# Attention of a two-layer block: head pairs on half rows, four heads' values in turn, and a reordered setup

## The reference

```
q = ln(x, lna_w) @ Wq.T + bq;  k = ln(x, lnb_w) @ Wk.T;  v = ln(x, lnb_w) @ Wv.T + bv
# q, k scaled by HD**-0.25 and split into 16 heads of HD = 8
for i in range(3):
    qp, kp, vp = qcur @ lq_w.T + lq_b, k @ lk_w.T + lk_b, v @ lv_w.T + lv_b
    sq, sk = ln(qp, lnc_w) * rsqrt(temp), ln(kp, lnd_w)
    scores = where(pos < cw, sq @ sk.T / sqrt(HD), -inf)
    iter_out = where(row < cw, softmax(scores) @ vp, 0)
    diff = mean(abs(iter_out - prev))            # sets the next window cw and the flags
    qcur = qcur + iter_out;  prev = iter_out
output = attn @ Wo.T + bo
```

## Time and profile before

| what | value |
|---|---|
| three runs | 592.22, 596.55, 597.31 us |
| median | 596.55 us |
| the profiled execution | 597.31 us, its span 595.6 us |
| mean granted clock of PE, share of full speed | 0.756 |
| PE, DVE, ACT, POOL busy | 373.8, 330.7, 180.8, 193.0 us |

### The profile page before, as it was taken

One profiled execution on the slowest core, in us unless ns is written; L12 is line 12 of the kernel. 1 busy time (PEld: TensorE's weight loads), 2 busy tenths in 40 slices (PEclk: granted clock), 3 DMA queues, 4 the chain that ended last, 5 costly groups with the idle time before them and its releaser, 6 DMA issues.

```text
span 595.6 us, 8658 instructions
## 1 busy us (share of the span) xinstructions
PE 373.8 (63%) x2164; PEld 262.0 (44%) x2165; DVE 330.7 (56%) x974; ACT 180.8 (30%) x376; POOL 193.0 (32%) x341
## 2 busy tenths in 40 slices
PE   1843698578981769249578999854506451049890
PEld 0631234424331333013378999843504451048890
DVE  7886797696019683000655555521576988126770
ACT  0020155103530114124225445411653054023540
POOL 8010003778895006730030000375120002714442
PEclk9965598556995558769978999965757855559996
DMA  2995000000000001110012222221153000233320
GB/s 59 272 362 188 0 0 2 1 0 2 0 0 0 0 1 36 53 44 0 10 53 56 60 66 70 71 66 48 40 187 148 1 0 10 100 88 79 77 65 2
DMA packets 36217, 34.55 MB, mean 58 GB/s; under 512 B 6259, under 2 KB 26949, under 8 KB 36192
## 3 DMA queue, kind: packets, MB, share of 16 engines
q1 hardware_dynamic: 32432, 26.83, 14.7%
q0 software_dynamic: 3712, 7.44, 4.4%
q10 hardware_dynamic: 48, 0.00, 0.0%
HBM read 19.92 MB, written 14.79 MB: 58 GB/s over the span
## 4 chain that ended last, share of the span: by engine, by line
PE 39%; issue 22%; DVE 19%; another core or an unknown queue 8%; DVEq 2%; ACT 2%; SPq 2%; DMA 2%; POOL 1%; ACTq 0%; POOLq 0%
PE ps L886 11%; PE ps L1001 8%; PE ps L1012 7%; DVE mx L1488 4%; PE ps L860 4%; PE ps L827 3%; PE ps L875 3%; SPq L284 2%; DVEq L1599 1%; DVE w_now L1604 1%; DVE rs_a L1127 1%; PE ps L991 1%; DMA y<-back,posu 1%; DVE rs_a L1126 1%
## 5 line engine op out<-in xcount | busy, mean ns | idle before, releaser
L460 POOL DMA_INDIRECT rows<-token_rows,posu x48 | 48.4, 1008 | 162.7 <-DVE posu L1419 82.9
L1001 PE MATMUL ps<-xsT,w_now 128*128 128x128 f32 x552 | 82.4, 297 | 23.5 <-issue 14.7
L1612 DVE TENSOR_TENSOR hb<-ps,b_in 128x512 f32<-128x512 f32 x69 | 47.5, 689 | 84.0 <-PE ps L1001 53.2
L886 PE MATMUL ps<-wide,v_now 128*32 128x309 f32 (+2 forms) x256 | 76.1, 440 | 22.2 <-ACT wide L597 10.5
L1001 PEld LDWEIGHTS ps<-xsT,w_now 128*128 128x128 f32 x552 | 73.5, 208 | 29.6 <-issue 17.7
L1012 PE MATMUL ps<-w_out,hg 128*128 x552 | 79.5, 292 | 6.0 <-issue 3.0
L1012 PEld LDWEIGHTS ps<-w_out,hg 128*128 128x128 f32 x552 | 72.7, 206 | 8.1 <-issue 8.0
L679 ACT ACTIVATE hg<-hb 128x512 f32<-128x512 f32 x69 | 43.3, 630 | 49.2 <-DVE hb L1612 46.5
L886 PEld LDWEIGHTS ps<-wide,v_now 128*32 128x32 f32 x256 | 25.7, 116 | 59.8 <-issue 20.6
L1488 DVE TENSOR_REDUCE mx<-ps 128x512 f32 (+2 forms) x48 | 43.5, 948 | 12.1 <-PE ps L860 12.1
L1454 DVE TENSOR_SCALAR den<-ps 128x48 f32<-128x48 f32 (+1 forms) x3 | 0.6, 203 | 87.6 <-PE ps L911 87.6
(11 more groups left out here) (335 smaller groups left out, 584.8 us busy)
## 6 DMA issues: line engine op xcount, KB each, us to landing
rows<-zeros SPq DMA_DIRECT2D x22, 256.0 KB, 6.3
xs<-rows SPq DMA_DIRECT2D x69, 64.0 KB
back<-ys SPq DMA_DIRECT2D x46, 64.0 KB
w_in<-in_L_ffn_w_fc SPq DMA_DIRECT2D x1, 2048.0 KB, 14.1
w_in<-in_L_ffn_W SPq DMA_DIRECT2D x1, 2048.0 KB, 8.5
rest<-rows SPq DMA_DIRECT2D x23, 65.0 KB
token_rows<-in_L_attn_x SPq DMA_DIRECT2D x1, 832.0 KB, 8.1
wmod<-in_L_wmod SPq DMA_DIRECT2D x2, 384.0 KB, 4.4
```

Source lines behind the costliest of these rows:

```text
L460: pool.indirect_dma_start(ROWS[l], bass.IndirectOffsetOnAxis(ap=posu[:, k, j:j + 1], axis=0), token_rows[:, j, 0:WIDTH[l]], None).then_inc ...
L886: mm = pe.matmul(ps[q * OROW:(q + 1) * OROW, 6, 0:nw], v_now[:, q, jk, :], probs[:, q % 2, jk, 0:nw], start=(jk == 0), stop=(jk == nj - 1))
L1001: mm = pe.matmul(ps[:, c % RING, n * P:(n + 1) * P], w_now[:, c % 2, n * P:(n + 1) * P], xsT[:, c % 2, :], start=True, stop=True)
L1612: v.tensor_tensor(hb[:, c % 2, :].rearrange("p (b t) -> p b t", b=NB), ps[:, c % RING, :].rearrange("p (b t) -> p b t", b=NB), b_in[:, l, ...
```

## The change

Keys and queries of a head pair lie on half rows. A head's keys take 64 rows (the head's half of the turned stack) and the scores product reads these alone (`half`); the key buffer holds 8 pairs instead of 16 heads, and isn't cleared first. The maxima are one bf16 number instead of three. The stack is turned by groups of four heads (`turn_group`), and the turns stand between the score products; ACT makes most of the copies. In the softmax, four heads' weighing products alternate for each key tile (`weigh_four`), with 9 columns each straight from `vpx`, into 8 exp buffers; the last group goes head by head. The output turn is a product with `omap`, 17 columns a head: values, sum of weights, and the values mapped by lq_w. DVE adds the mapped values straight to the mapped queries `qp` (`next_queries`); scaling, the sum of differences, window and masks come behind the query stack. All attention loops are written out. The inverse root has 8 operations for 10. In the setup the head maps are merged into the projection matrices, biases come in by products, POOL's small constants go first. Counting and placing of "far" move into iteration 1's softmax and with them the scatter; gate weights move from iteration 0's to iteration 2's; rotations are computed by vectors over all powers, the two longest by DVE in iteration 2.

```diff
@@ tensor
-            def turn_stack(name, nj):
-                for g in range(4):
-                    for a in range(2):
-                        for j in range(nj):
...
+            def turn_group(g, bank, nj, name):
+                for a in range(2):
+                    for j in range(nj):
+                        at = j * HEADS + 4 * g + 2 * a
+                        mm = pe.transpose(psb[:, bank, a * NATT + j * P:a * NATT + (j + 1) * P],
+                                          stack[:, at:at + 2, :].rearrange("p h s -> p (h s)"), identb[:])
+                mm.then_inc(sem(name), 1)
...
+                def half(t, h):
+                    return t[STK * (h % 2):STK * (h % 2) + STK, h // 2, :]
...
-                with pe.Fori(0, HEADS // 2) as i:
-                    for b in range(2):
-                        pe.wait_ge(sem("max_free"), 2 * i + (HEADS * it + b + 1))
-                        for j in range(nj):
-                            mm = pe.matmul(ps[:, 3 * b + j, 0:nw], qs[:, bass.ds(i, 1), j * P:(j + 1) * P],
-                                           ks[:, bass.ds(2 * i + b, 1), 0:nw], start=True, stop=True)
...
+                            mm = pe.matmul(ps[:, 3 * b + j, 0:nw], half(qs, h)[:, j * P:(j + 1) * P], half(ks, h)[:, 0:nw], start=True, stop=True)
...
+                def weigh_one(g, q, jk):
+                    h = 4 * g + q
+                    return pe.matmul(ps[OROW * q:OROW * q + HD + 1, 6 + g % 2, 0:nw], vpx[:, jk, h, :], probs[h % NPROBS][:, jk, 0:nw],
+                                     start=(jk == 0), stop=(jk == nj - 1))
+                def weigh_four(g, jk):
...
+                        pe.wait_ge(sem("probs_ready"), H0 + 4 * g + 4)
+                    for q in range(4):
+                        mm = weigh_one(g, q, jk)
...
+                for g in range(3):
+                    weigh_four(g, 0)
+                    scores_t(4 * g + 6, 4 * g + 7)
+                    weigh_four(g, 1)
+                    scores_t(4 * g + 7, 4 * g + 8)
+                    if nj == 3:
+                        weigh_four(g, 2)
+                    if it == 1 and g == 0:
+                        count("far")
+                    if g < 2:
+                        scores_t(4 * g + 8, 4 * g + 10)
@@ vector, between two iterations
-                attention_scaled(it)
-                signal(v.tensor_reduce(asum[:], af, AX.X, ALU.add, apply_absolute_value=True), "asum", it + 1)
-                v.wait_ge(sem("attT"), it + 1)
-                signal(v.tensor_tensor(qT[:], qT[:], ps[:, 5, 0:NATT], ALU.add), "qT", it + 2)
+            def next_queries(it):
+                nj = -(-WINDOWS[it] // P)
+                r = weights_of(it)
+                gs = grouped(gl_s, nj)
+                then(v.tensor_tensor(gs.rearrange("p (j h) o -> p j h o", h=HEADS), outputs(it)[:, :, :, HD + 1:OW], r, ALU.mult))
+                then(v.tensor_tensor(grouped(qp, nj), grouped(qp, nj), gs, ALU.add))
+                return r
@@ gpsimd
-            pool.memset(ks[:, :, :], 0.0).then_inc(sem("ks_zero"), 1)
```

More of the change, by code:

```diff
@@ L266, in build_adaln @@
         ROWS = {0: rows0, 1: rows1}
-        TURN_BANK = {"far": 0, "near": 3}
+        TURN_BANK = {"far": 3, "near": 3}
+        LOGIT_BANK = {"far": 5, "near": 2}
+        COUNT_AT = {"far": ((7, 0), (7, 256)), "near": ((3, 0), (4, 0)), "all": ((3, 0), (4, 0))}
         def tiles_before(l):
@@ L496, in _ @@
             then(pool.memset(roty[H:P, 0:1], -1.0))
+            pool.wait_ge(sem("ks_act"), 4)
+            for k, p0 in enumerate((0, STK)):
+                pool.memset(ks[p0:p0 + 1, :, WINDOWS[1]:NATT], MASKED).then_inc(sem("ks_masked"), 1)
+                pool.wait_ge(sem("ks_masked"), k + 1)
             pool.wait_ge(sem("sines"), 1)
-            then(pool.tensor_copy(turn[:, 0:1], ph[:, 7:8]))
-            then(pool.tensor_copy(turn[:, 1:2], ph[:, 6:7]))
-            c_, s_, cc, ss, t_ = (turn[:, k:k + 1] for k in range(5))
@@ L600, in take @@
-                def take(i):
-                    act.wait_ge(sem("probs_free"), 4 * i + (HEADS * it + 6))
-                    act.wait_ge(sem("oT_clear"), 1)
-                    act.copy(oT[:, bass.ds(i, 1), 0:nw], ps[:, 6, 0:nw]).then_inc(sem("o_taken"), 1)
-                for q in range(4):
-                    head(0, q)
-                with act.Fori(0, HEADS // 4 - 1) as i:
-                    head(i + 1, 0)
-                    take(i)
-                    for q in range(1, 4):
-                        head(i + 1, q)
@@ new lines, in attend, with longest_rotations @@
+                gate_weights(0)
+                gates("far")
+                longest_rotations()
+            def longest_rotations():
+                v.wait_ge(sem("rotations"), 1)
+                for m in (NPOW - 2, NPOW - 1):
+                    L = 1 << m
+                    n = min(L, N + 1 - L)
+                    c, sn = turn[:, 0, m:m + 1], turn[:, 1, m:m + 1]
+                    X, Y, tc, ts = rotx[:, 0:n], roty[:, 0:n], tmp_c[:, 0:n], tmp_s[:, 0:n]
+                    then(v.tensor_scalar(tc, Y, sn, None, ALU.mult))
+                    then(v.tensor_scalar(ts, Y, c, None, ALU.mult))
+                    then(v.scalar_tensor_tensor(out=rotx[:, L:L + n], in0=X, scalar=c, in1=tc, op0=ALU.mult, op1=ALU.subtract))
+                    then(v.scalar_tensor_tensor(out=roty[:, L:L + n], in0=X, scalar=sn, in1=ts, op0=ALU.mult, op1=ALU.add))
@@ L1670, in experts @@
                     bias_down(0, t - 2, e[t - first])
-            for it in range(3):
-                attend(it)
+            r = attend(0)
+            r = attend(1, r)
+            attend(2, r)
             experts(0)
```

767 lines of the change are left out of this document (414 added, 353 removed).

## The result

The changed kernel took 531.11 us (four runs, 525.35 to 532.66) against 596.93 for the kernel before (four runs, 592.22 to 600.16, three of them those of the first table); the ratio is 0.8885, with a 95% interval of 0.880 to 0.898. The profiled execution took 531.3 us, its span 529.5. Forecast were 506.1. The sign held and so did the wide range (486 to 538), which took in the rivals; the forecast's own range, 496 to 516, was missed by 15 us.

A forecast was written before the change was run, and what follows sets the result against it. No engine was taken to bound the whole; DVE- and PE-bound stages follow without overlap. Stage terms summed to -91.2 us from 597.3, giving 506.1; own range 496 to 516, wider range with rivals 486 to 538.

The forecast's parts named there:

- the stall: Iteration 2, exp to output: 24 us of unexplained waits, blamed on hardware loops beside indirect DMAs and taken as gone.
- Stages, not busy time: Whole span: no engine bounds it, so the sum was made stage by stage and not by busy time.
- Setup, -15.2: Start of kernel to first query stack: 52.2 us before, 15.2 us shorter by three pieces removed.
- its three pieces: Setup: POOL's memset and queue order 4, merged projection and head maps 6.3, key copies and norm 4.7 us gone.
- Between iterations, -12.5: Last output's turn to next query stack, twice: five DVE operations ahead of the norm, -4.9 and -7.6 us.
- Maxima, +8.9: Maxima stages of three iterations: turns between scores and small DVE copies add 2.3, 3.3 and 3.3 us.
- six of the turns stand between the scores: Maxima stages: each such turn costs 0.3 to 0.5 us at the low clock, part of the added time.
- Exp to output: First exp to turned output: iterations 0, 1 and 2 to take 16.1, 23.6 and 25.5 us, -8.2, -12.6 and -36.7.
- two side by side: Weighing, exp to output: neighbouring passes of different column groups overlap in pairs, 12.5 us for iteration 2's 96 passes.
- a rival: Half clock, exp to output: PE granted 0.50, 552 us; it shared a chance of 0.12 with no column-group overlap.
- stall kept: Rival, chance 0.22: the stall belongs to the indirect DMAs and moves with the scatter into iteration 1, +24, 530 us.
- 8 us of straight code beside them without one: Before iteration 2's loops, 226.5 to 234: the same indirect DMAs cost nothing, the argument against the stall being kept.

The follow-up runs named there:

- e12: Changed kernel with the turns of the first three groups of maxima put behind all score products, on a chip without the waits; 478.6 us.
- e1: Changed kernel without the 26 indirect DMAs that scatter the far rows; 475.8 us, on a chip where the kernel before took 546.1.
- e2: Changed kernel with each far-scatter DMA issued only when the one before has landed, on a chip without the waits; 475.2 us.
- e3: Changed kernel with DVE's gate weights moved from iteration 2's softmax to the end of iteration 1's, far scatter unpaced, on a chip without the waits; 477.2 us.
- e5: Changed kernel as it is, run again on another chip that had the waits; 516.1 us against 593.4 for the kernel before, ratio 0.872.
- e6: Kernel before as it is, traced on a later group's chip that had the waits; 592.6 us.
- e8: Changed kernel with the far scatter's DMAs one at a time, on a chip with the waits; 501.5 us, 14.6 less than unpaced there.
- e11: Kernel before, loops untouched, with the far scatter one DMA at a time, on a chip without the waits; 572.8 us, 26 slower than unpaced.
- e10: Changed kernel with far scatter, near scatter and gathers all one DMA at a time, on a chip without the waits; 521.4 us.

## Why the prediction was right, and where it was off

The direction is as forecast, and most of the size: the setup, the steps between stages and iteration 2 came as worked out. The step that failed is the stall, taken as gone.

- **Stages, not busy time.** Right. The steps between the stages gave 15.9 + 12.7 us and the setup 13.7, though PE was busy for 63% of the span before and 62% after.
- **Setup, -15.2.** Measured -13.7. It was read as a whole; its three pieces (which add up to 15.0, where the sum has 15.2) weren't tested.
- **Between iterations, -12.5.** Measured -12.7: five operations ahead of the norm, the rest under the turns, and the first maximum no later (5.0 and 5.5 us behind the stack; what the prediction calls PE's start, 5.3 to 5.7, is this maximum, PE itself started 0.4 to 0.6 behind the stack before the change and 0.05 in iteration 2 after it).
- **Maxima, +8.9.** Measured +0.9. The step that failed is "six of the turns stand between the scores" as a cost on top. DVE waits 0.4 to 0.5 us once for a group's turn, but the 0.23 that it waited before with every second head is gone within a group, and the two nearly cancel. Gap and maxima together, e12 shows the interleaving to be worth 0.6 us in iteration 1 and some 2 in all three.
- **Exp to output.** The length of iteration 2 was right, 24.8 for 25.5, and for a partly wrong reason: "two side by side" was mis-sized, since four run so, and the clock was taken as before, where it starts at 0.50 and comes up late (0.51 over iteration 1's first 12.7 us). That the two errors cancel in iteration 2, and in iteration 1 where there are no waits (23.3 to 26.4 in e1, e2 and e3, for 23.6), is luck. In iteration 0, which is short, they don't: 20.1 for 16.1. That the clock might be lower than before was in no step of the prediction as a term, only in a rival. Across the runs with the same order of PE's work this stage took 19.8 to 22.5 us, with clocks of 0.59 to 0.50.
- **The stall, -24.** This step failed: "I take the stall as one of loops beside indirect DMAs, and so gone." It came back in straight code: iteration 1 took 28 us more than forecast, with the scatter beside it. The rival "stall kept" (0.22) had the mechanism and gave 530 for the 531 measured; that it came within 1 us is luck, since the maxima were 8 us better than forecast, and the wait itself, iteration 0 and the rest after attention 4 each worse. The argument for loops was "8 us of straight code beside them without one"; the changed kernel has such a start too (121.96 to 130.6, with no late signal over 1.3 us), so it was the start of a burst, not the kind of code.
- **Size of the change by chip.** Of the 91.2 us forecast, 24 were the stall. Without them the forecast is 67; a waitless chip shows 546.1 to 477.2 (e3, nearest to the changed kernel), 69 less. The first measurement gave 66, since its wait only moved; e5 gave 77, where it also got shorter.

The Trainium skill's rule on taken branches ("Runtime: NRT & Kernel Launch", section "Instruction fetch mechanics") doesn't explain it: waits of 13 us stood where there is no branch. e3, which was to tell whether fetch of any kind is late, ran where there are no waits; the queues of the two stalls, shown with the result, speak against it.

What stays open is the mechanism. Shown is that signals of PE to ACT and DVE come late, while ACT's to PE came in 0.05 us at the same time; that this is found beside indirect DMAs one every 1.27 to 1.4 us and not beside the far ones at one every 2.5 us; that its first unexplained piece in the chain of the kernel before begins 9 us (e6: 11.5) into the far scatter, in the changed kernel ACT's wait 8.6 us into it, and in the near scatter 3.0 us into it (the changed kernel, e5, e8); that the last late start is 1 to 4 us behind the burst; and that the first measurement and one of the three later groups have it. The three groups ran on three chips and none of these twice, so whether it belongs to the chip or to its state on the day isn't known. In e5 a signal from DVE to PE was late once as well (2.2 us), so it isn't PE's alone. The scattered rows themselves weren't late there: SyncE, which waits for them all, went on at 155.44, 2.3 us after the last issue at 153.18.

## What to carry to other kernels

A wait that no engine explains, beside a burst of indirect DMAs, is to be read by the burst: compare its start and end with the first and last late signal, look whether instructions were being fetched, and try one DMA at a time before changing the code that waits. Pacing is free only where the transfer starts well ahead of its reader; put in the chain it costs 1.0 to 1.3 us a DMA (26.3 us for 26 in e11, 43.0 for 32 in e10). And where a matrix product is made faster in a stage whose clock starts low, ask what the engine waits for next, since that wait, or a lower clock, may take back what the packing gives.

## What was not expected of the hardware

The kernel before differs by 47 to 51 us (546 against 593 to 597) from one group of runs to another (three chips, and the first measurement's isn't on record), and in e6 the waits account for all of it. Four matrix products of 9 columns in four column groups start within 0.02 us of each other and go on 0.26 apart. And the granted clock can differ between kernels with the same order of PE's work in the same stage, 0.50 or 0.59, on one chip too (e5 and e8).
